# A graph network on one Trainium2 core: the squares of the first attention go partly to GpSimd

## The reference, cut to what matters

```python
z = xx @ W_fc.T
e = jax.nn.sigmoid(jnp.concatenate([z[src], z[dst]], axis=-1) @ W_attn.T)
emax = jax.ops.segment_max(e, dst, num_segments=n)
w = jnp.exp(e - emax[dst])
denom = jax.ops.segment_sum(w, dst, num_segments=n)
h = jax.ops.segment_sum(w / denom[dst] * z[src], dst, num_segments=n)
```

## Time and profile before

| | |
|---|---|
| median of 3 runs | 9600.13 us (9592.98 to 9600.5) |
| the profiled execution | 9602.42 us |
| its span | 9600.4 us |
| busy in the span | PE 4956.7, VectorE 4621.7, ScalarE 2822.2, GpSimd 5429.7 us |
| first VectorE and last TensorE work on attend's pieces | about 4706 and 5588 us from the start |

### The profile page before, as it was taken

One profiled execution on the slowest core, in us unless ns is written; L12 is line 12 of the kernel. 1 busy time (PEld: TensorE's weight loads), 2 busy tenths in 40 slices (PEclk: granted clock), 3 DMA queues, 4 the chain that ended last, 5 costly groups with the idle time before them and its releaser, 6 DMA issues.

```text
span 9600.4 us, 77317 instructions
## 1 busy us (share of the span) xinstructions
PE 4956.7 (52%) x27910; PEld 2738.6 (29%) x27910; DVE 4621.7 (48%) x6121; ACT 2822.2 (29%) x2192; POOL 5429.7 (57%) x5420
## 2 busy tenths in 40 slices
PE   1000008998257777765577656344430005539977
PEld 0000007887013233221222223234420003233334
DVE  5677877776000000000498930588875301529860
ACT  0111110000000000000498920366667400519840
POOL 3777767777777777777600036788877777020000
PEclk5555555555678988987798979676665557759988
DMA  8666626443598998999799988455569716938767
GB/s 184 217 216 220 220 62 148 155 146 132 205 414 362 410 366 362 415 363 415 249 282 272 288 211 322 148 205 198 200 234 376 247 49 227 377 87 288 263 212 270
DMA packets 1228866, 2404.25 MB, mean 250 GB/s; under 512 B 566568, under 2 KB 818923, under 8 KB 1197595
## 3 DMA queue, kind: packets, MB, share of 16 engines
q1 hardware_dynamic: 1022714, 2076.35, 61.0%
q0 software_dynamic: 187136, 170.29, 6.8%
q10 hardware_dynamic: 18720, 153.79, 4.0%
HBM read 1606.44 MB, written 711.62 MB: 241 GB/s over the span
## 4 chain that ended last, share of the span: by engine, by line
POOL 36%; DMA 26%; issue 12%; PE 12%; ACT 6%; ACTq 3%; DVE 3%; DVEq 1%; SPq 1%; POOLq 0%
POOL arena L483 17%; DMA arena<-cells_w 14%; POOL xd L486 9%; POOL cells_w L486 8%; DMA arena<-cells_c 8%; PE ps L696 5%; ACT arena L1006 4%; ACTq L1005 3%; ACT arena L1004 2%; PE ps L776 2%; DMA arena<-cells_turned 2%; PE ps L861 1%; DMA arena<-hot 1%; PE ps L1137 1%; PE ps L1029 1%
## 5 line engine op out<-in xcount | busy, mean ns | idle before, releaser
L696 PE MATMUL ps<-arena 128*64 128x458 f32 (+2 forms) x7252 | 1343.3, 652 | 704.0 <-DMA arena<-cells_w 702.5
L483 POOL DMA_INDIRECT arena<-t_a,arena x832 | 940.1, 1130 | 1101.7 <-DMA t_a<-arena 848.5
L1029 PE MATMUL ps<-arena 128*33 128x400 f32 x6336 | 1161.5, 521 | 313.0 <-DVE arena L1024 305.3
L486 POOL DMA_INDIRECT sorted<-arena x832 | 844.2, 1015 | 289.1 <-issue 289.1
L714 DVE COPY carry<-ps 64x128 f32<-64x128 f32 (+1 forms) x5 | 1.5, 295 | 2045.3 <-PE ps L696 2045.3
L486 POOL DMA_INDIRECT xd<-arena x832 | 832.8, 1001 | 258.0 <-issue 253.2
L486 POOL DMA_INDIRECT cells_c<-arena x832 | 810.6, 974 | 292.8 <-issue 292.8
L486 POOL DMA_INDIRECT cells_w<-arena x832 | 812.6, 977 | 276.8 <-issue 276.8
L483 POOL DMA_INDIRECT arena<-t_kv,idx x832 | 817.0, 982 | 258.7 <-issue 253.2
L696 PEld LDWEIGHTS ps<-arena 128*64 128x64 f32 (+1 forms) x7252 | 425.7, 147 | 1618.6 <-issue 851.2
L861 PE MATMUL ps<-arena 128*96 128x400 f16 x2368 | 520.2, 373 | 424.4 <-DMA arena<-cells_c 217.5
(11 more groups left out here) (530 smaller groups left out, 9154.9 us busy)
## 6 DMA issues: line engine op xcount, KB each, us to landing
arena<-cells_w SPq DMA_DIRECT2D x245, 3200.0 KB, 18.1
arena<-cells_c SPq DMA_DIRECT2D x290, 800.0 KB, 5.2
arena<-cells_turned SPq DMA_DIRECT2D x200, 800.0 KB, 8.4
cells_w<-arena SPq DMA_DIRECT2D x49, 3200.0 KB, 20.9
weighed_cells<-arena SPq DMA_DIRECT2D x68, 1600.0 KB, 14.3
arena<-weighed_cells SPq DMA_DIRECT2D x68, 1600.0 KB, 7.3
cells_c<-arena SPq DMA_DIRECT2D x50, 1600.0 KB, 5.8
cells_turned<-arena SPq DMA_DIRECT2D x100, 800.0 KB, 5.4
```

The source lines that it names most:

```text
L483: return pool.indirect_dma_start(dst, None, table, bass.IndirectOffsetOnAxis(ap=index, axis=0))
L486: return pool.indirect_dma_start(table, bass.IndirectOffsetOnAxis(ap=index, axis=0), source, None)
L696: mm = pe.matmul(bank[base + k][g * f:(g + 1) * f, 0:m], rows_of, tile[:, g * width + at:g * width + at + m], start=first, stop=last, skip ...
L1029: last = pe.matmul(bank[4 * h + c][64 * kind:64 * kind + 33, 0:400], own[:, t, :], moving[:, 400 * c:400 * c + 400], start=t == 0, stop=do ...
```

## The change

In attend, from source tile 14 on (the fifteenth) in phase 1 and in all of phase 0, every odd piece (b = 1 and b = 3) is squared by GpSimd; ScalarE squares the even ones, as before; VectorE squares none there. In the first 14 tiles of phase 1, and in "back", nothing changes. GpSimd waits for `weights_made` of its piece. VectorE waits for GpSimd's `squared` between its multiplication and its last operation on such a piece.

```diff
+        POOL_FROM = 14
...
-        def squared_late(b):
-
-            return b == 3
+        def squared_by(name, phase, t, b):
+
+            if name == "attend" and (phase == 0 or t >= POOL_FROM):
+                return "pool" if b % 2 else "act"
+            return "dve" if b == 3 else "act"
+
+        def squares_pool(pool):
+
+            for k, _, b, _, phase, t, h in pieces("attend", (0, 1)):
+                if squared_by("attend", phase, t, b) == "pool":
+                    tanh = TANH["attend"][b]
+                    pool.wait_ge(S["weights_made"], k + 1)
+                    pool.tensor_tensor(tanh, tanh, tanh, ALU.mult).then_inc(S["squared"], 1)
...
-                if not squared_late(b):
+                if squared_by(name, phase, t, b) == "act":
                     last = act.activation(tanh[b], tanh[b], ACT.Square)
...
-                if squared_late(b):
+                by = squared_by(name, phase, t, b)
+                if by == "dve":
                     dve.tensor_tensor(tanh[b], tanh[b], tanh[b], ALU.mult)
                 dve.drain()
+                if by == "pool":
+                    squares[0] += 1
+                    dve.wait_ge(S["squared"], squares[0])
                 dve.scalar_tensor_tensor(tanh[b], tanh[b], -1.0, expo[b], ALU.add, ALU.mult).then_inc(S["weighed"], 1)
...
             sort_pool(pool)
+            squares_pool(pool)
```

More of the change, by code:

```diff
@@ L1006, in weigh_act @@
                 last = act.activation(expo[b], tanh[b], ACT.Exp, scale=0.5, bias=half[:])
-                if not squared_late(b):
+                if squared_by(name, phase, t, b) == "act":
                     last = act.activation(tanh[b], tanh[b], ACT.Square)
                 last.then_inc(S["weights_made"], 1)
+        squares = [0]
         def weigh_dve(dve, name, phase):
             expo, tanh = EXPO[name], TANH[name]
-            for k, _, b, i, _, _, h in pieces(name, (phase,)):
+            for k, _, b, i, _, t, h in pieces(name, (phase,)):
                 p, n = read_of(name, i)
```

## The result

The change makes the kernel slower. Its median is 9706.23 us (4 runs, 9697.17 to 9711.73), against 9596.56 us for the kernel before, run beside it on the same chip (4 runs). The ratio is 1.0114, with a 95% interval of 1.0097 to 1.0132: about 110 us more. The direction and the mechanism are those forecast; the forecast size was 185 us.

The account below looks back on a forecast made before the run. ScalarE (8.58 us a tile) and SyncE's queue (about 8.6) were taken as bounds. With 7.28 + 3.4 + 0.1 = 10.78 us, 84 x (10.78 - 8.58) = 185 us more gave 9785 us; range 9640 to 9870.

Parts of the forecast that it names:

- main case: 84 changed tiles of attend: VectorE's operations and GpSimd's square exclude each other, 9734 to 9844 us; chance 0.70.
- P: Length of one GpSimd square of 1600 columns, taken as 3.4 us, between 2.8 and 4.1.
- light exclusion: Rival: GpSimd blocks for single reads only, or squares nearly as quickly as one stream; P = 1.45 gives 9621 us; chance 0.12.
- Exclusion in both directions: In a changed tile, VectorE's two-input operations and GpSimd's square each wait for the other, whoever goes first.
- an instruction of GpSimd: Read from the sort's DMAs: one starting during VectorE's operation on two SBUF tiles stands still until that is over.
- 7.28 + P + a handover: Time of a changed tile: VectorE's own 7.28 us, one square and 0.1 us handover, 10.78 us against 8.58.
- handover of 0.1: Gap between VectorE's work and GpSimd's square in a tile, 0.1 us, about that between two VectorE operations.
- no exclusion, and the queue sets the pace: Rival: GpSimd reads beside VectorE, SyncE's queue stays at 8.6 us a tile; 12 us less, 9588 us; chance 0.12.
- The rival in which the whole 60 us appear: No exclusion, and SyncE's queue follows ScalarE's faster pace in both phases: 9542 us; chance 0.06.

Follow-up runs that it names:

- the two runs that come nearest to it: Against the changed kernel: GpSimd fills its 84 pieces with a constant, 0.9992 of before; nobody squares from the fifteenth tile on, 0.9987 of before.
- three buffers alone: Kernel before, with three buffers in place of two for transposing DMAs, the next issued before the last's store: 0.9996, 9594.57 us.
- the better division alone: Kernel before, with VectorE squaring 5 of 16 pieces of attend in place of 4, ScalarE 11, GpSimd none: 0.9997, 9610.13 us.

## Why the prediction was right in kind and too large

**The time is inside the range, but not inside the case that was to bring it.** The main case, exclusion with a P of 2.8 to 4.1 us, was given as 9734 to 9844 us. 9706 us lies below it, in the stretch that the prediction had left to "light exclusion", and there with a chance of 0.12 only. The mechanism of the main case is nevertheless the one that the runs show: VectorE stands still for almost the whole of a square. That the measured time fell inside the stated range is in part luck, since the range reached down there for another reason.

**Exclusion in both directions** was right. Rows of before showed only GpSimd waiting for VectorE; the other direction was an assumption, with the Trainium skill's rule beside it ("SBUF — State Buffer", section "Who interferes with whom"). The runs show it, and show that it is the reading that counts: a fill of the same width blocks nothing. It isn't held back either, and takes 1.43 us each of the 84 times beside a busy VectorE, so the prediction's "an instruction of GpSimd" was too wide. "For the whole instruction", as the prediction puts the rule, is too strong where GpSimd comes first: VectorE's own 1.82 us began 0.14 us before a square's end, and 1.12 us before the end of a `tensor_scalar`. The measurement decides. All of VectorE's operations in these pieces have two SBUF inputs; how one with a single SBUF input fares beside a square was not tried.

**"7.28 + P + a handover"** held as a form, over 42, 84 and 168 squares. **Its P of 3.4 us and handover of 0.1 were the step that failed.** Together they should have been 2.58. The square's whole length alone is 2.85 us, and the blocked part is shorter: VectorE goes on 0.14 us before its end, and its beginning can run beside VectorE's operation before, as in the second place above. I had put the three streams half in turn. The rate in the rows of iota fits: a column of a square takes 1.66 ns, twice 0.834, and two streams of 1600 columns at that rate are 2.67 us, the measured 2.58 within 4%. That the write lies beside the reads is inferred from this; that a write blocks nothing is shown by the fill. With 2.58 the sum is 84 x (9.86 - 8.58) = 108 us, and 110 were measured. So close an agreement is partly chance: in the profiled executions the two phases grew by 105 us, and what lies around them moved by 4 and 7 us. The lower of the two ends, 2.8, was the nearer one.

The prediction's estimate of 3.5 us for the square, from the Trainium skill, "GPSIMD Engine Reference", section "Performance versus the Vector engine", was too long: the trace has 2.85 alone and 3.36 as the median, waits for VectorE included. The measurement decides.

**The pieces**: long operations of 5 us were forecast, 4.41 came; a tile of 10.8 us, 9.87 came; phase 0 longer by 108 us and phase 1 by 77, 61 and 44 came; ScalarE at 74%, 78% came. All are the same wrong term: with 2.58 us the two phases would be 49 x 1.28 = 63 and 35 x 1.28 = 45 us longer.

**That nothing else stood in the way** was right: GpSimd came free in time, and the wait for `squared` costs nothing (the run without it has the same time). TensorE's granted clock did sink, from 0.97 to 0.89 in phase 0, but VectorE still fills 98% of the stretch, so it did not bind.

**The rival "no exclusion, and the queue sets the pace"** can now be priced: 0.08% (not clear of zero) and 0.13% below before in the two runs that come nearest to it, where 12 us (0.13%) had been worked out. Its reading of the chain of waits was sound. The rival in which the whole 60 us appear is refuted: even leaving out all squares brings 12 us by the medians, and no more than 21 by its interval.

## What to carry to other kernels

An idle GpSimd is no free engine beside a VectorE that works on two SBUF inputs: work that reads there is paid by VectorE, here at 2.58 us for what VectorE does itself in 1.73. Price an offload by the time it blocks, not by the busy share it takes away, and look in the trace before for instructions of GpSimd that end a fixed time after VectorE's.

Where two bounds have the same pace, freeing either gave nothing that could be measured here, and both had to be freed in one step to see the gain: three buffers alone 0.04%, the better division alone 0.03%, both 0.3%.

## What the runs showed that I had not expected

A one-input operation of GpSimd (`tensor_scalar`, 1600 fp32 columns) takes 4.24 us, 1.5 times as long as its two-input product of the same width (2.85 us), and blocks VectorE for 2.98 us in place of 2.58. So the time for which VectorE stands still is not set by how much GpSimd reads. That it is set by how long GpSimd goes on reading fits all the runs, and isn't shown by itself.

Of a `tensor_tensor` on GpSimd, 1600 columns take 2.85 us and 800 take 1.52 at the shortest: 1.66 ns a column, and about 0.2 us fixed. A `memset` of 1600 columns takes 1.43 us, each time, beside a busy VectorE.
